# A first layer norm that is no longer applied to x: centred projection weights, and the inverse deviations carried by V and the sums column

## What is computed

```
h   = (x - mean) / sqrt(var + 1e-5)            # over the 128 features
q, k, v = split(h @ w_qkv)                      # 16 heads of 8
w   = relu(q k^T / sqrt(8));  w = w / (sum(w) + 1e-6)
y   = h + (w v) @ w_out + b_out
x1  = x + layernorm(y) * gamma + beta
h2  = layernorm(x1)
out = x1 + sqrt((h2 @ cos(theta + theta_noise))^2 + (h2 @ sin(phi + phi_noise))^2)
```

## Time and profile before

| | |
|---|---|
| median of three runs | 439.32 us |
| the profiled execution | 439.75 us, span 438.0 us |
| TensorE (PE) busy | 427.1 us, 98% |
| VectorE (DVE) busy | 338.2 us, 77% |
| ScalarE (ACT) busy | 342.5 us, 78% |
| GpSimd (POOL) busy | 40.4 us, 9% |
| granted TensorE clock | 0.998 of full speed |

### The profile page before, as it was taken

How to read it: one execution, slowest core, us unless ns; L and a number is a source line. 1 busy time by engine, 2 the same in 40 slices (tenths; PEclk the granted TensorE clock), 3 DMA queues, 4 the chain that set the end, 5 groups by cost and what they waited for, 6 DMA issues and landing times.

```text
span 438.0 us, 9143 instructions
## 1 busy us (share of the span) xinstructions
PE 427.1 (98%) x3366; PEld 131.3 (30%) x3366; DVE 338.2 (77%) x693; ACT 342.5 (78%) x598; POOL 40.4 (9%) x52
## 2 busy tenths in 40 slices
PE   8899999999999999999999999999999999999985
PEld 6332222222223232222223232222223232222244
DVE  6775788778687967877777967878787977877757
ACT  2767888788787878888888878888887878888843
POOL 4793000000000001000000001000000001000001
PEclk9999999999999999999999999999999999999999
DMA  5027821000010000101010000101010000000000
GB/s 162 25 52 154 168 63 25 1 19 7 1 26 0 25 1 3 49 0 25 1 26 1 25 1 1 49 0 26 1 26 1 0 1 1 25 0 3 1 1 25
DMA packets 6810, 11.27 MB, mean 26 GB/s; under 512 B 1648, under 2 KB 3312, under 8 KB 6384
## 3 DMA queue, kind: packets, MB, share of 16 engines
q1 hardware_dynamic: 6624, 10.56, 10.0%
q10 hardware_dynamic: 144, 0.13, 0.1%
HBM read 1.77 MB, written 1.05 MB: 6 GB/s over the span
## 4 chain that ended last, share of the span: by engine, by line
PE 92%; DVE 3%; ACT 3%; DMA 1%; POOL 0%; issue 0%; DVEq 0%
PE pv L932 57%; PE sc L899 26%; PE pv L939 3%; PE pv L980 1%; PE pv L831 1%; PE pv L840 1%; DMA x_sb<-x_dram 1%; PE pv L852 1%; PE pv L953 1%; ACT w_buf L482 1%; ACT w_buf L479 1%; DVE stats L586 0%; DVE x L720 0%; PE sc L939 0%; PE sc L980 0%
## 5 line engine op out<-in xcount | busy, mean ns | idle before, releaser
L932 PE MATMUL pv<-w_buf,v_sb 128*32 128x512 f32 x2048 | 272.3, 604 | 0.0
L632 DVE TENSOR_SCALAR w_buf<-sc 128x512 f32<-128x512 f32 x256 | 177.0, 691 | 79.0 <-PE sc L899 68.6
L479 ACT ACTIVATE w_buf<-sc 128x512 f32<-128x512 f32 x256 | 153.2, 598 | 74.8 <-PE sc L899 74.6
L482 ACT ACTIVATE w_buf<-sc 128x512 f32<-128x512 f32 (+1 forms) x256 | 185.1, 723 | 0.0
L899 PE MATMUL sc<-q_rep,k_rep 32*128 32x512 f32 x1024 | 135.0, 494 | 1.7 <-ACT w_buf L479 0.9
L636 DVE TENSOR_SCALAR w_buf<-sc 128x512 f32<-128x512 f32 x179 | 121.8, 680 | 0.8 <-PE sc L899 0.8
L899 PEld LDWEIGHTS sc<-q_rep,k_rep 32*128 32x128 f32 x1024 | 53.0, 181 | 216.4 <-ACT w_buf L479 167.7
L932 PEld LDWEIGHTS pv<-w_buf,v_sb 128*32 128x32 f32 x2048 | 40.4, 108 | 65.2 <-ACT w_buf L482 29.1
L406 POOL TENSOR_TENSOR x<-x,mv 128x512 f32<-128x512 f32 (+1 forms) x5 | 4.4, 885 | 309.6 <-DVE x L720 309.6
L860 PE MATMUL pv<-ident 128*128 128x128 f32 x64 | 9.7, 324 | 1.5 <-POOL ident L352 1.5
L860 PEld LDWEIGHTS pv<-ident 128*128 128x128 f32 x64 | 9.4, 238 | 1.5 <-POOL ident L352 1.5
(11 more groups left out here) (107 smaller groups left out, 153.5 us busy)
## 6 DMA issues: line engine op xcount, KB each, us to landing
q_rep<-q_hi SPq DMA_DIRECT2D x30, 64.0 KB, 2.1
q_rep<-q_lo SPq DMA_DIRECT2D x30, 64.0 KB, 2.1
k_rep<-k_hi SPq DMA_DIRECT2D x6, 256.0 KB, 4.1
k_rep<-k_lo SPq DMA_DIRECT2D x6, 256.0 KB, 5.5
x_sb<-x_dram SPq DMA_DIRECT2D x3, 256.0 KB, 4.0
out_dram<-x SPq DMA_DIRECT2D x3, 256.0 KB, 2.7
k_rep<-k_hi SPq DMA_DIRECT2D x6, 64.0 KB, 2.1
k_rep<-k_lo SPq DMA_DIRECT2D x6, 64.0 KB, 2.1
```

The source lines that it names most:

```text
L479: nc.scalar.activation(w_buf[:, s % W_STEPS, 0, :], early[:, 0, :], ACT.Relu).then_inc(relu[0], 1)
L482: nc.scalar.activation(w_buf[:, s % W_STEPS, 2:2 + n, :], late[:, 0:n, :], ACT.Relu).then_inc(relu[0], 1)
L632: nc.vector.tensor_scalar(w_buf[:, s % W_STEPS, 1, :], early[:, 1, :], 0.0, None, ALU.max).then_inc(relu[1], 2 if both else 1)
L932: last = nc.tensor.matmul(bank[32 * i:32 * i + 32, :], v_sb[:, k, HPG * g + i, :], w_buf[:, s % W_STEPS, i, :], start=(k == 0), stop=(k == ...
```

## The change

The layer norm of x is taken out of the way of the projections. Its mean is put into the weights: with C = I - 1/128, (x - mean) W = x (C W). So raw x is transposed, and TensorE multiplies w_qkv by the matrix centring = C once. Its deviation is put elsewhere. q and k stay unscaled by 1/std; a key's two factors (from k and from v) go into V as inv_var, the sums column carries the root of inv_var instead of ones, and a query's factor cancels, but for the small constant, which becomes DEN_EPS times that query's std (eps_std).

In detail:

- Chunk 0 of x comes in one transfer, issued by ScalarE; w_qkv is the first transfer of SyncE.
- VectorE splits statistics(c) from variance(c), does not normalise chunk 0 any more, and copies the centred weights from PSUM (take_weights). Chunk 2's statistics move into the steps.
- take_v is five operations: one Sqrt into the sums column and a scaled copy for each tile.
- All four roots (for h and eps_std) go behind steps 12 and 13 of group 0, and GpSimd normalises all four chunks after them. x_beta is gone: its values are made in x_sb itself.

The diff's core:

```diff
             def _(pool):
                 nc.gpsimd.memset(ident[:, :], 0.0).then_inc(ident_zero, 1)
+                nc.gpsimd.memset(averager[:, :], 1 / D).then_inc(averager_ready, 1)
...
+                pool.wait_ge(ident_ready, 1)
+                pool.wait_ge(averager_ready, 1)
+                nc.gpsimd.tensor_tensor(centring[:, :], ident[:, :], averager[:, :],
+                                        ALU.subtract).then_inc(centring_ready, 1)
...
-                normalise_x(1)
-                normalise_x(2)
-                pad_v(1)
-                normalise_x(3)
-                for g in range(2, G):
+                for g in range(1, G):
                     pad_v(g)
-                nc.gpsimd.memset(averager[:, :], 1 / D).then_inc(averager_ready, 1)
+                pool.wait_ge(rstd_ready, NC)
+                nc.gpsimd.tensor_tensor(eps_std[:, :], var_eps[:, :], rstd[:, :], ALU.mult).then_inc(std_ready, 1)
+                pool.wait_ge(std_ready, 1)
+                nc.gpsimd.tensor_scalar(eps_std[:, :], eps_std[:, :], DEN_EPS, None,
+                                        ALU.mult).then_inc(eps_std_ready, 1)
                 for c in range(NC):
-                    nc.gpsimd.tensor_tensor(x_beta[:, chunk(c), :], x_sb[:, chunk(c), :], means(c),
+                    normalise_x(c)
+                pool.wait_ge(xn_ready, NC)
+                pool.wait_ge(xT_done, NC + 1)
+                for c in range(NC):
+                    nc.gpsimd.tensor_tensor(x_sb[:, chunk(c), :], x_sb[:, chunk(c), :], means(c),
                                             ALU.subtract).then_inc(x_centred, 1)
...
                 def take_v(c):
                     act.wait_ge(v_done, c + 1)
-                    nc.scalar.copy(v_sb[:, chunk(c), :, 0:HD],
-                                   v_bank[c].rearrange("p (t h d) -> p t h d", t=TPC, h=H)).then_inc(v_ready, 1)
+                    act.wait_ge(var_ready, c + 1)
+                    nc.scalar.activation(v_sb[:, chunk(c), :, HD],
+                                         inv_var[:, chunk(c)].unsqueeze(2).to_broadcast([P, TPC, H]), ACT.Sqrt)
+                    for t in range(TPC):
+                        n = c * TPC + t
+                        last = nc.scalar.activation(v_sb[:, n, :, 0:HD],
+                                                    v_bank[c][:, t * P:(t + 1) * P].rearrange("p (h d) -> p h d", h=H),
+                                                    ACT.Copy, scale=inv_var[:, n:n + 1])
+                    last.then_inc(v_ready, 1)
...
-                run_pass(0, [((0, 0), lambda: take_k(1)), ((0, 1), lambda: take_xT(2)), ((0, 2), lambda: root(3)),
+                run_pass(0, [((0, 0), lambda: take_k(1)), ((0, 1), lambda: take_xT(2)),
...
+                             ((0, 12), lambda: root(0)), ((0, 12), lambda: root(1)),
+                             ((0, 13), lambda: root(2)), ((0, 13), lambda: root(3)),
...
                 statistics(0)
-                normalise_x(0)
+                variance(0)
+                take_weights()
                 statistics(1)
-                statistics(2)
...
-                run_pass(0, [((0, 0), lambda: take_k(1)), ((0, 1), lambda: statistics(3)),
+                run_pass(0, [((0, 0), lambda: take_k(1)), ((0, 0), lambda: variance(1)), ((0, 1), lambda: statistics(2)),
+                             ((0, 2), lambda: variance(2)), ((0, 4), lambda: statistics(3)),
+                             ((0, 4), lambda: variance(3)),
...
                 transpose_first()
+                pe.wait_ge(centring_ready, 1)
+                pe.wait_ge(wqkv_loaded, 16)
+                nc.tensor.matmul(sc[2][:, 1, 0:3 * D], centring[:, :], wqkv_sb[:, :], start=True,
+                                 stop=True).then_inc(w_centred, 1)
+                transpose_x(1)
                 pe.wait_ge(xT_ready, 2)
```

More of the change, by code:

```diff
@@ L95, in block_kernel @@
         xn = sb("xn", [P, NT, D])
-        x_beta = sb("x_beta", [P, NT, D])
         xT = sb("xT", [P, NT * P])
@@ L133, in block_kernel @@
         rstd = sb("rstd", [P, NT])
+        var_eps = sb("var_eps", [P, NT])
+        eps_std = sb("eps_std", [P, NT])
+        centring = sb("centring", [P, P])
         stats_p = sb("stats_p", [P, TPC, 6])
@@ L168, in block_kernel @@
         ln_own = sem("ln_own")
+        stats_own = sem("stats_own")
         var_ready = sem("var_ready")
@@ L399, in _ @@
                     pool.wait_ge(x_centred, c + 1)
-                    nc.gpsimd.tensor_tensor(x_beta[:, chunk(c), :], x_beta[:, chunk(c), :], row(beta_b, TPC),
+                    nc.gpsimd.tensor_tensor(x_sb[:, chunk(c), :], x_sb[:, chunk(c), :], row(beta_b, TPC),
                                             ALU.add).then_inc(xb_ready, 1)
@@ L460, in take_head @@
                     nc.scalar.copy(head[:, :], bank).then_inc(ready, 1)
-                act.dma_start(x_sb[:, 2:TPC, :], x_v[:, 2:TPC, :]).then_inc(x_second, 16)
-                root(0)
+                act.dma_start(x_sb[:, 0:TPC, :], x_v[:, 0:TPC, :]).then_inc(x_loaded[0], 16)
                 for half in range(2):
@@ L583, in statistics, with variance @@
                     for t in range(c * TPC, (c + 1) * TPC):
-                        if t == 2:
-                            dve.wait_ge(x_second, 16)
                         last = nc.vector.bn_stats(stats[:, t, :], x_sb[:, t, :])
-                    own(last)
+                    last.then_inc(stats_own, 1)
+                def variance(c):
+                    dve.wait_ge(stats_own, c + 1)
                     for t in range(c * TPC, (c + 1) * TPC):
@@ L590, in statistics @@
                     own(last)
-                    own(nc.vector.tensor_scalar_add(inv_var[:, chunk(c)], mv[:, chunk(c), 1], LN_EPS))
-                    nc.vector.reciprocal(inv_var[:, chunk(c)], inv_var[:, chunk(c)]).then_inc(var_ready, 1)
-                def normalise_x(c):
-                    dve.wait_ge(rstd_ready, c + 1)
-                    for t in range(c * TPC, (c + 1) * TPC):
-                        nc.vector.tensor_scalar(xn[:, t, :], x_sb[:, t, :], mv[:, t, 0:1], rstd[:, t:t + 1],
-                                                ALU.subtract, ALU.mult).then_inc(xn_tile, 1)
+                    own(nc.vector.tensor_scalar_add(var_eps[:, chunk(c)], mv[:, chunk(c), 1], LN_EPS))
+                    nc.vector.reciprocal(inv_var[:, chunk(c)], var_eps[:, chunk(c)]).then_inc(var_ready, 1)
                 def low_part(lo, hi, hi_ready, lo_ready, c, bank, turn):
@@ L644, in normalise @@
                     dve.wait_ge(pvT_done, m + 1)
-                    own(nc.vector.tensor_scalar_add(den[:, tiles, :], pvT[:, :, :, HD], DEN_EPS))
+                    first_tile = (c - (g == G - 1) if c is not None else NC - 1) * TPC
+                    own(nc.vector.tensor_tensor(
+                        den[:, tiles, :], pvT[:, :, :, HD],
+                        eps_std[:, first_tile + tiles.start:first_tile + tiles.stop].unsqueeze(2).to_broadcast(
+                            [P, n, HPG]), ALU.add))
                     own(nc.vector.reciprocal(den[:, tiles, :], den[:, tiles, :]))
@@ L721, in first_residual @@
                             out=x1[:, t, :], in0=y[:, t, :], scalar=rs_p[:, t:t + 1],
-                            in1=x_beta[:, bass.ds(part.j * TPC + t, 1), :].rearrange("p o d -> p (o d)"),
+                            in1=x_sb[:, bass.ds(part.j * TPC + t, 1), :].rearrange("p o d -> p (o d)"),
                             op0=ALU.mult, op1=ALU.add)
@@ L749, in run_pass @@
                             relu_step(c, NT * g + k)
+                            if k == 3 and c == 0 and g == 1:
+                                dve.wait_ge(eps_std_ready, 1)
                             if k == 3 and not c == g == 0:
@@ L800, in transpose_first @@
                     for t in range(TPC):
-                        pe.wait_ge(xn_tile, t + 1)
-                        last = nc.tensor.transpose(xT_bank[0][:, t // 2, t % 2 * P:(t % 2 + 1) * P], xn[:, t, :], ident[:, :])
+                        if t == 0:
+                            pe.wait_ge(x_loaded[0], 16)
+                        last = nc.tensor.transpose(xT_bank[0][:, t // 2, t % 2 * P:(t % 2 + 1) * P], x_sb[:, t, :], ident[:, :])
                         if t % 2:
@@ L819, in transpose_x @@
                     for t in range(TPC):
-                        last = nc.tensor.transpose(xT_bank[c][:, t * P:(t + 1) * P], xn[:, c * TPC + t, :],
+                        last = nc.tensor.transpose(xT_bank[c][:, t * P:(t + 1) * P], x_sb[:, c * TPC + t, :],
                                                    ident[:, :])
```

42 lines of the change are left out of this document (19 added, 23 removed).

## The result

The changed kernel takes **445.80 us** (median of 4 runs, 445.39 to 446.48), against 439.38 for the kernel before on the same chip: a ratio of 1.0145, with a 95% interval of 1.0133 to 1.0158. The forecast was 443.4, with a range of 440.4 to 445.5; the result lies 0.3 above the range. The profiled execution took 445.39 us, span 443.3, 5.3 more than before's.

A forecast was written before the change was run, and what follows sets the result against it. The prediction took TensorE's own queue, busy 98% of the span, as the bound. A head term of +1.37 and collisions of +2.75 made +4.1 on 439.32, so 443.4 us, range 440.4 to 445.5.

The forecast's parts named there:

- TensorE's start of the head: First head projection, after warm-up, transposes and centring matmul: to start at 8.1 to 8.4, against 8.35 before.
- starvation: Rival: VectorE's trig operations are kept out until GpSimd's back-to-back additions end; +4.4 there, 445.1 us in all; chance 0.06.
- ScalarE behind q_head: Head: table load 1.28, Sqrt 0.15 and four copies 1.12 precede ScalarE's first relu, then at 13.2 to 13.5.
- d: Head: lateness of k_hi(1) behind ScalarE's work after q_head, +0.05 to +0.4, taken as +0.25 us.
- gap case: Rival: ScalarE stands still beside the table load for up to 1.28 more; 444.7 with the lock, 442.0 without; chance 0.08.
- variance(1): VectorE, between k_lo(1) and the relu of step 1: delays score step 2's late half, TensorE paying all 0.74.
- take_v(1): ScalarE: grows from 0.59 to 1.40, so k(2), which waits for it, runs at 19.34, not 19.20: +0.14.
- k_lo(3): VectorE, step 5: relus start 0.7 late behind statistics(3) and variance(3), k_lo(3) ends at 25.84, k(0) waits: +0.24.
- den: VectorE: now a tensor_tensor of 16 columns, in idle time; in the tail at most 0.05.
- The collisions: GpSimd's additions (57.3 to 67.2) block VectorE's trig operations at add_noise, in_turns and whole_turns: +2.75, bounds 0 and 4.4.
- The lock does not bite: Rival: GpSimd yields or VectorE's operations run beside it, so only the head's +1.37 counts: 440.7 us; chance 0.24.
- The head wins: Rival: table load runs ahead of q_head, ScalarE free before first scores end; 438.9 to 439.6 without the lock; chance 0.09.

The follow-up runs named there:

- e4: The changed kernel with a one-column Sqrt as ScalarE's first activation, so the Sqrt table loads at the start and not behind q_head; 444.42 us.
- e7: The kernel before with GpSimd's eight additions held until score step 24 of pass 0, so they run beside the trig operations; 441.69 us.
- e13: e10 with GpSimd's additions put back beside the trig operations, where the change has them; 441.49 us.
- e3: The changed kernel with GpSimd's eight additions waiting for angles_ready, so none runs beside the trig operations; 443.36 us.
- a1: The changed kernel without any edit, profiled in a second execution; 446.86 us.
- e9: The kernel before with statistics(3) moved ahead of the relu of step 1 on VectorE, so TensorE stands still before score step 2's late half; 443.50 us.
- e10: The changed kernel with late memsets, additions behind angles_ready, Sqrt table first, variance(1) behind the head's low_rows_of for q, take_k(1) one step later; 439.15 us.
- e11: e10 with 9 warm-up matmuls instead of 12; 438.86 us.
- e5: The changed kernel with variance(1) ahead of take_k(1) in VectorE's queue behind step 0; 445.32 us.
- e1: The changed kernel with GpSimd's memsets of V for groups 1 to 3 started only after VectorE has copied w_rep; 444.92 us.
- a2: The changed kernel without any edit, profiled in a third execution; 445.63 us.
- e2: The changed kernel with GpSimd waiting for the end of each memset of V before starting the next; 445.46 us.
- e6: The changed kernel with five more warm-up matmuls on TensorE between chunk 1's transposes and the first head projection; 447.10 us.
- e8: The changed kernel with memsets late, additions behind angles_ready, Sqrt table first and variance(1) ahead of k_lo(1), all at once; 439.95 us.

## Why the prediction was wrong

**The sum, term by term.**
- *TensorE's start of the head* was forecast at 8.1 to 8.4. Where VectorE is in time it is 8.16 on average: right. In the change's profile it is 9.15. **This is the step that failed**: "GpSimd makes the centring matrix beside the warm-up: nothing to pay" looked at what GpSimd delivers, and "four small memsets that nobody waited for" at what falls away, but not at what the weight copies, the normalisations and GpSimd's waits ahead of them had done: they stood between the long memsets and kept the first apart from the rest. (The small memset did not: see the next point.) The price is 1.0 us in executions where VectorE gets in last (four profiles of seven without an edit there), and about nothing in those where it gets in after two memsets.
- *The evidence against starvation was misread.* The rival had a chance of 0.06, for the additions alone, because "L579 ended at 2.91, 0.17 after the long memset, though GpSimd had a second one queued right behind". GpSimd's timeline of the kernel before has the second one:

```profile
2.68 0.21 POOL L358 MEMSET v_sb<- 128x64 f32 x1
```

  It ends at 2.89, and L579 ends 0.02 after it, just as low_rows ends 0.02 after the last memset now. VectorE had not been let in between; it had been held through both, and the second was short. The trace of before thus held the starvation, at a price of 0.2.
- *ScalarE behind q_head*: table load, Sqrt and four copies gave 3.06 from q_head to the first relu, forecast 3.12; the load followed 0.01 after q_head. From the first scores to k_hi(1) are 2.59 instead of 1.88: 0.71, where the forecast's d of 0.25 and first scores 0.6 earlier made 0.85. The gap case fell (e4: the load was worth 1.03, where a gap of its own length would have made 0.97 + 1.28).
  The Trainium skill ("ScalarE: Activation LUTs", What ACT_TABLE_LOAD costs) adds a drain of about 1.38 us to a load; the trace disagrees, with idle times of 0.01 ahead of the load and 0.02 behind it.
- *variance(1)* 0.75 (forecast 0.74), *take_v(1)* 0.11 (0.14), *k_lo(3)* 0.19 (0.24), den nothing: right.
- *The collisions* were right in kind and too dear in size: 1.96 in the trace where 2.75 stood. Of the three places two were hit. add_noise cost 0.84 more than before, in_turns 0.29 and 1.10, together 2.23, of which some 0.3 fell into idle time. whole_turns, the third place with 1.55 of the forecast, ran at 69.55, just behind the last addition, which ended at 69.45, and paid nothing. The sum had let blocking stretch the additions by about a microsecond; all eight took 10.10, against 9.9 without blocking, and so they were over. In exchange GpSimd took its turn between the two operations of in_turns, though the second waits for no semaphore: the 0.5 put there was the middle of 0 and 1.1, and it is 1.1. The pairs of medians give 2.1 (e7), 2.3 (e13) and 2.4 (e3).
  By the Trainium skill ("SBUF — State Buffer", Who interferes with whom) the engine that issues first keeps the shared ports for its whole instruction and the other blocks. The stretched operations agree with it: each ended once one addition had. In the 5.21 us of low_rows VectorE was blocked through four memsets in a row.
- *No term for TensorE's clock.* The forecast put 1 us more of waiting ahead of score step 2 and took it that a wait costs its own length. It costs 1.4 to 2.9 more when the clock falls behind it (the change's profile; a1, 1.47 dearer; e9).

**The sum as it came out**, in the profiled execution: 0.29 + 0.71 + 0.75 - 0.05 + 0.11 + 1.39 + 0.19 - 0.01 + 1.96 = 5.34, at the tail, against 4.1. Of the excess of 1.2, the two missing terms make 2.3 (held VectorE 0.9, as the first scores came at +0.29 and not at -0.6; clock 1.39); the collisions, put 0.8 too high, and 0.3 in the small terms of the head stand against them. So it is partly luck that the forecast came as near as it did: with the collisions at their measured 1.96 the sum would have been 442.6. Of the signs that the prediction named, the load directly behind q_head and the stretched trig operations came; the late scores of step 2 (17.95, not 17.2 to 17.4) and k(0) (29.82, not about 27.8) did not. By medians the change costs 6.42, by the two profiled executions 5.64; a1, with a fall twice as long, shows where such a difference comes from.

**The other rivals.** "The lock does not bite" is refuted by e3 and e7. "The head wins" needed ScalarE free before the first scores end; even in e4 they end at 13.05 and ScalarE is free only at 13.17. With the load, the memsets, variance(1) and the additions moved, e10 does win, by 0.49, about the rival's best case of 0.45; e11, with three warm-up matmuls less, wins by 0.78.

## What to carry to other kernels

When an edit takes work out from between others on GpSimd, ask what that work had kept apart: VectorE may need the gap. Look at whom a blocked instruction actually ended behind, to 0.01 us, before taking it as evidence that it got in. A wait put in front of dense TensorE work can cost far more than its length, if the clock falls (in e9 a delay of 1.44 cost 4.34); so remove such stand-stills first (in e5 0.85 was enough), and look at the mean granted clock of executions before comparing their times.

## What the runs showed of the hardware

- **VectorE can be held through several GpSimd instructions.** The same two-column tensor_scalar, behind the same four memsets of 1.3 us, took 2.67 or 5.21 us; with a wait of GpSimd after the first memset it was 1.41 in all eight profiles that had one. The tensor_scalar of variance(0), 0.17 in e1 with no memset beside it, took 0.72 in a2 and 1.01 in e2 and ended 0.02 after the last memset, while the batch-norm statistics beside the same memsets kept their 0.87. What decides when it is let in stays open. Against tensor_tensor additions on GpSimd each operation was let in after one.
- **The granted clock falls at a stand-still of TensorE or just behind it, but not always.** Twelve profiles have a wait of 0.85 to 2.24 us ahead of score step 2's late half (the change's three, e1's two, e2 to e6, e8, e9). In eight of them the clock fell to 0.50, from 0.8 us before the wait ended to 1.5 us after; e1 in its first profile, e2, e3 and e8 did not fall there. With waits of 0.35 to 0.70 (before, e7, e10 to e13) none did. The low stretches last 3.4 or 6.8 us and cost 1.4 or up to 2.9. What picks the moment and the length was not found.
- **The mean granted clock of an execution goes with its time.** e3: 1.000 gives 441.92, 0.996 gives 443.22, 0.994 gives 443.50, 0.990 gives 443.81. e7, with 1.000 four times, spreads over 0.14 us. It is no exact order: in e2 0.992 gives 446.64 and 0.991 gives 445.40. (Down to 0.997 it can be the idle tail alone: before has such executions at its usual time.)
- **The warm-up, 24 matmul records that never change, takes 4.42 to 5.49 us**, with 1.00 shown as the granted clock throughout. In the change's profile a window of 1 us holds 6 or 7 of the records up to 5.0 and 9 from 5.0 to 6.0; in a1 it holds 6 or 7 up to 7.0. So the pace rises at a different time, and the clock shown does not tell the two paces apart.
